# Moving VectorE's query cosine product between query and key normalisation, and GpSimd's sine products behind it

## The reference, cut to what matters

```
for i in range(6):
    x = attn_layer(shift_tokens(x), Wqkv[i], ...) + x
    x = ffn_layer(shift_tokens(x), ...) + x

def attn_layer(x, ...):                   # 16 heads of 64, windows of 32 tokens
    q, k, v = split(x @ Wqkv)             # 3 x 1024 columns
    q = l2norm(q) * qs
    k = l2norm(k) * ksc
    q = q * cos * scale + rotate_half(q) * sin * scale
    k = k * cos * inv   + rotate_half(k) * sin * inv
    out = local_attention(q, k, v)        # each window sees itself and the one before
    return out @ Wo
```

## Time and profile before

| | us |
|---|---|
| median of 3 runs | 4559.74 |
| lowest and highest | 4546.97, 4564.44 |
| profiled execution, its own time | 4569.05 |
| span of the profiled execution | 4567.3 |
| VectorE busy (83%) | 3773.8 |
| TensorE busy (88%) | 4022.1 |
| ScalarE busy (57%) | 2591.2 |
| GpSimd busy (45%) | 2047.5 |

### The profile page before, as it was taken

The page is one execution under the profiler, slowest core; times in us unless marked ns, Lnnn a source line. Parts: engine busy times, 40 slices in busy tenths (PEclk is TensorE's granted clock), DMA queues, the critical chain, the costliest instruction groups (busy, mean ns, idle before and its releaser), DMA issues. The chain is left out here.

```text
span 4567.3 us, 113436 instructions
## 1 busy us (share of the span) xinstructions
PE 4022.1 (88%) x42352; PEld 3105.1 (68%) x42352; DVE 3773.8 (83%) x7539; ACT 2591.2 (57%) x4144; POOL 2047.5 (45%) x1530
## 2 busy tenths in 40 slices
PE   5998989989989989938858869989899899899998
PEld 4866867858758768615535558668578587686685
DVE  7998989979989889745324289899899899898996
ACT  4756747747647657512412457567477476475674
POOL 5644536535546456230010055456356454564561
PEclk9999999999999999968968989999999999999999
DMA  2111111111111111130030011111111111111111
GB/s 60 26 41 23 28 34 29 27 37 27 27 36 27 38 25 27 17 98 2 1 83 1 1 47 26 40 25 27 40 23 28 38 26 34 31 27 40 24 27 23
DMA packets 436340, 142.15 MB, mean 31 GB/s; under 512 B 413009, under 2 KB 419153, under 8 KB 433873
## 3 DMA queue, kind: packets, MB, share of 16 engines
q1 hardware_dynamic: 434608, 131.33, 13.7%
q10 hardware_dynamic: 1152, 3.15, 0.3%
HBM read 38.72 MB, written 1.05 MB: 9 GB/s over the span
## 5 line engine op out<-in xcount | busy, mean ns | idle before, releaser
L917 POOL TENSOR_TENSOR pool<-pool 128x512 f32<-128x512 f32 x768 | 1174.6, 1559 | 1171.1 <-DVE pool L961 1170.9
L529 PE MATMUL psum<-squares,pool 128*128 128x128 f32 x3072 | 699.8, 275 | 49.4 <-ACT pool L787 20.6
L531 PE MATMUL psum<-squares,pool 128*128 128x128 f32 x3072 | 694.4, 273 | 0.0
L740 ACT ACTIVATE pool<-psum 128x1024 f32<-128x1024 f32 x384 | 394.1, 1026 | 387.0 <-PE psum L458 387.0
L563 PE MATMUL psum<-pool 128*64 128x128 f32 x6144 | 549.0, 293 | 22.1 <-DMA pool<-pool 19.6
L456 PE MATMUL psum<-wqkv_hi,xs_lo 128*128 128x512 f32 x1152 | 524.4, 455 | 26.9 <-DVE pool L961 19.2
L760 ACT COPY pool<-psum 64x512 f32<-64x512 f32 x768 | 448.4, 584 | 175.4 <-PE psum L531 169.9
L529 PEld LDWEIGHTS psum<-squares,pool 128*128 128x128 f32 x3072 | 433.3, 141 | 110.2 <-ACT pool L787 46.8
L945 DVE TENSOR_REDUCE pool<-pool 128x16 f32<-128x1024 f32 x384 | 452.5, 1212 | 45.6 <-ACT pool L740 39.9
L921 POOL TENSOR_TENSOR pool<-pool 128x1024 f32<-128x1024 f32 x192 | 458.7, 2389 | 0.0
L457 PE MATMUL psum<-wqkv_lo,xs_hi 128*128 128x512 f32 x1152 | 457.2, 397 | 0.0
(11 more groups left out here) (169 smaller groups left out, 7822.3 us busy)
## 6 DMA issues: line engine op xcount, KB each, us to landing
pool<-pool SPq DMA_DIRECT2D x768, 64.0 KB, 2.5
pool<-pool SPq DMA_DIRECT2D x192, 128.0 KB, 2.4
pool<-in_wqkv SPq DMA_DIRECT2D x12, 1536.0 KB, 6.1
k_st<-turn_st SPq DMA_DIRECT2D x8, 1536.0 KB, 21.0
pool<-in_wo SPq DMA_DIRECT2D x12, 512.0 KB, 3.3
pool<-in_w SPq DMA_DIRECT2D x12, 341.0 KB, 3.0
pool<-in_w SPq DMA_DIRECT2D x12, 192.0 KB, 3.0
rotary<-in_rotary SPq DMA_DIRECT2D x2, 1024.0 KB, 5.1
```

Of the source, the lines that this page charges most:

```text
L529: pe.matmul(o, by_cos[:, p // 2, 2 * c:2 * c + 2, :], ident, start=True, stop=False, is_transpose=True)
L531: last = pe.matmul(o, by_sin[:, p // 2, 2 * c:2 * c + 2, :], ident, start=False, stop=True, is_transpose=True)
L917: last = g.tensor_tensor(by_sin[:, q, :, hd * r:hd * r + hd], qn[:, q, :, hd * (1 - r):hd * (2 - r)], tab, ALU.mult)
```

## The change

VectorE's query cosine product moves from behind the key normalisation to between the two, with the residual, which stood between key normalisation and cosine, ahead of it. GpSimd's first sine product of a unit waits for it (`cos_ready`) besides what it waited for. At a layer's end `hidden(3, 2)` now stands behind both normalisations and the cosine, and the wait for the tables ahead of them.

```diff
@@ gpsimd, step @@
                                 for q in range(2):
                                     g.wait_ge(qn_ready, done(U, 2, q))
+                                    if q == 0:
+                                        g.wait_ge(cos_ready, done(U))
                                     g.wait_ge(t_ready, done(U - 1, 4, 2 * q + 1))
@@ vector @@
-                    def normalise_qk(U):
+                    def normalise_qk(U, t, between=None):
...
                             v.tensor_tensor(qn[:, q], bank(2 * q, 2).rearrange("p (h e) -> p h e", e=DH),
                                             nwt[3][:, HEADS * q:HEADS * (q + 1)].unsqueeze(2)
                                             .broadcast_to([P, HEADS, DH]), ALU.mult).then_inc(qn_ready, 1)
+                            if q == 0:
+                                if between:
+                                    between()
+                                cosine(U, t)
 
                     def cosine(U, t):
 
-                        v.wait_ge(qn_ready, done(U, 2, 1))
+                        v.wait_ge(qn_ready, done(U, 2, 0))
@@ vector, step @@
                             if k == 1:
                                 norms(U)
-                                normalise_qk(U)
-                                cosine(U, 0)
+                                normalise_qk(U, 0)
...
                                 norms(U, between=probabilities(U - 2) if has(2) else ())
-                                normalise_qk(U)
-                                if has(3):
-                                    residual(U - 3, i, k - 3)
-                                cosine(U, 2 * i + k // 2)
+                                normalise_qk(U, 2 * i + k // 2,
+                                             (lambda: residual(U - 3, i, k - 3)) if has(3) else None)
@@ vector, the layer's end @@
-                            normalise_qk(N0)
+                            v.wait_ge(turn_ready, done(l + 1 + L0))
+                            normalise_qk(N0, 0)
                             hidden(3, 2)
-                            v.wait_ge(turn_ready, done(l + 1 + L0))
-                            cosine(N0, 0)
@@ vector, the start of a half @@
                     norms(L0 * UNITS)
-                    normalise_qk(L0 * UNITS)
                     v.wait_ge(turn_ready, done(L0))
-                    cosine(L0 * UNITS, 0)
+                    normalise_qk(L0 * UNITS, 0)
```

## The result

The changed kernel takes **4658.85 us** (median of 4 runs, 4649.38 to 4659.24) against 4554.01 for the kernel before (4 runs by now, 4546.97 to 4564.44): the ratio is 1.0218, with a 95% interval of 1.0191 to 1.0245. That is 105 us more by the medians and 99 by the ratio. The profiled execution took 4649.38 us, the lowest of the four.

The account below looks back on a forecast made before the run. VectorE was taken to bound the unit at 15.67 us. Middle units' 75 us plus layer ends' 15 made 90 us, so 4650 us against the median of 4559.74; range 4595 to 4672.

Parts of the forecast that it names:

- Where the two meet: Middle units: L152 waits for GpSimd's key cosine product until 10.70; period 16.15 against 15.67, 75 us over 156 units.
- the first rival: Middle units: only L152 is held, L153 and later steps slip past GpSimd's copy; 0.20 us a unit, 4606 us; chance 0.12.
- The order on VectorE: Middle units: the cosine no longer waits for GpSimd's sine product, so VectorE gains 1.06 us a unit before L152.
- the new wait: GpSimd's first sine product starts at 3.23 instead of 1.45, its key cosine product runs from 8.30 to 10.70.
- Other waits: Later-freed key banks of PSUM stay hidden from TensorE by some 0.4 us; key squares and scores are early enough; no cost.
- The end of a layer: Last hidden product starts 1.48 us late in ten layers with a successor, nothing absorbs it: 15 us.
- The rival with TensorE's own chain as the bound: L152 and GpSimd's key cosine product never meet; TensorE's 15.67 us bounds the unit: 4560 to 4575, no slowdown; chance 0.12.
- The one with TensorE following VectorE: VectorE keeps its 1.06 us a unit and TensorE, only paced by VectorE, speeds up too: 4410 us; chance 0.04.

Follow-up runs that it names:

- The halved product: Changed kernel with GpSimd's key cosine product made for 8 of 16 heads only, the rest left out: 4584.88 us, 1.0053.
- the kernel with the wait alone: Kernel before, old order kept, with only GpSimd's wait for the query cosine product added: 4734.76 us, 1.0393.
- both terms treated: Changed kernel, hidden product moved between query normalisation and cosine, plus GpSimd's wait removed (4591.09 us, 1.0061) or its key cosine product split in two (4558.6, 1.0007).

## Why the prediction was right

The forecast was 4650 us and slower; measured were 4658.85. The added time was forecast as 90 us and measured as 99 by the ratio, 105 by the medians. That the total is nearer than that, by 6 us, is luck: the kernel before stood at 4559.74 with three runs and at 4554.01 with four.

*Where the two meet*: right in every part. L152 at 8.88 (forecast 8.88), GpSimd's key cosine product ending at 10.76 (10.70), L152 at 10.80 (10.74), the rest of the unit 5.40 (5.41), the period 16.20 (16.15). The term came to 73 us in the profiled execution, forecast 75, though made up a little differently: about 0.5 in each of units 3 to 13, 0.4 in unit 2 and 0.2 in unit 14. L153 is held as in the earlier trace rows, 0.42 us, which was the first rival's question, and it is out. What made this possible is that the kernel before held a unit in which the cosine happened to escape; it had already shown that the microsecond won is given back at L152.

*The order on VectorE* and *the new wait*: the gain is 1.05 (1.06), the start of GpSimd 3.28 (3.23). The halved product shows that L152's length is the GpSimd instruction's.

*Other waits*: TensorE does wait for the key banks now, since it runs ahead of the slower VectorE; the median is 0.25 us a middle unit, 0.60 in the one shown. The forecast had it hidden outright, by 0.4 us; it shows, but within the 0.5 us a unit that TensorE has to spare:

```profile
572.31 0.50 PE L456 MATMUL psum<-wqkv_hi,xs_lo 128*128 128x512 f32 x1 [0.60 <-DVE pool L963]
```

*The end of a layer* is **the mis-sized term**: forecast 15 us, measured 28. The lateness of the hidden product was right (1.37 for 1.48), and that the path behind it has no slack. What failed is the silent assumption that the work behind the longer idling takes as long as before. TensorE's ran at the lower clock, and the next sum of squares came 2.3 us late instead of 1.4. VectorE's then gave 0.7 back: GpSimd was through by that time, and L152 and L153 took 0.18 us each instead of 0.57 and 0.53. So the first unit came to 15.0 instead of 13.15 in eight of the ten layers, and to 16.2 in the two in which the clock stayed down longest. The second units' 5 us and the 2 us of the halves' first layers were in no term. The moved product in the changed kernel took 11 to 15 us back, not the whole 28.

The rival with TensorE's own chain as the bound had its size right, 15.64 to 15.68 where VectorE was relieved by a shorter GpSimd instruction (15.74 without the wait), but not its condition: in the changed kernel VectorE was not relieved. The one with TensorE following VectorE falls with the 0.48 us that VectorE waits for it. The advice of the Trainium skill on the shared access (SBUF — State Buffer, the summary of rules for kernel authors) holds here in its first half, that the second to come blocks: L152 ended 0.04 us behind GpSimd's product. The second half did not help: holding the idle engine back only moved the collision.

## What to carry to other kernels

Where two engines exclude each other by whole instructions, an idle engine's long instruction can cost the other engine all that is left of it, however small the step that meets it: look up what the other engine does at the time to which the work is pushed, and if they meet, cut the long instruction in two (the cut by itself, in the old order, was not tried). When a contention is taken away at one place, follow both engines in time to where they next meet. A unit in the trace in which the contention happened to be absent says what removing it is worth. And a remedy should be tried on the kernel before too: the moved hidden product helped both kernels, and only that comparison shows that the change kept a cost. Where a step is moved behind others, count what the engine that waits for it will do after a longer idle time, its clock too.

## What the runs showed of the hardware

VectorE's turn comes at the boundary between two GpSimd instructions even when these follow without a gap: a 128x32 step that waits 1.9 us for one 128x1024 product waits 0.84 and then 0.72 for the same work in two, and in the kernel with the wait alone L152 slipped in between two different products (0.69) while the step after it took the 1.83. Splitting cost GpSimd 0.13 us.

TensorE's granted clock fell around an idle time of 3.09 us at the hidden product in ten layers of ten (changed kernel; 38 of 40 with the three other kernels that have this idle time), and around 1.51 us there in none of ten (before; none of 20 with the wait alone). The longest idle time doesn't settle it: it also fell within 14 us of the query normalisation in six layers of ten, in each of the two kernels with both terms treated, where no idle time was above 2.8 us, and in two layers of ten of the kernel before behind waits of at most 1.9 us. At the lower level a 512-column product took 0.63 instead of 0.40 us, and the sum of squares came nearly 1 us later than the hidden product's delay alone would make it (2.3 against 1.37).
